# Holding results back while the second chunk of sorted tokens is gathered, and other orders at the attentions' last steps

## What is computed

```python
x = x + attention(layernorm(x), ...)
x = x + ffn(layernorm(x), ...)          # of each token:
    probs = softmax(xt @ Wr + br); gate = max(probs); idx = argmax(probs)    # 8 experts
    h = relu(layernorm_affine(xt) @ W1[idx] + b1[idx])                       # 128 -> 512
    y = (h @ W2[idx] + b2[idx]) * gate
```

## Time and profile before

| | |
|---|---|
| median of three runs | 680.22 us (679.19 to 682.71) |
| the profiled execution | 682.75 us, of it the span 681.4 us |
| PE busy | 652.9 us, 96% |
| ACT busy | 535.7 us, 79% |
| DVE busy | 476.1 us, 70% |
| POOL busy | 364.7 us, 54% |
| HBM read, written | 19.93 MB, 44.75 MB |
| mean granted TensorE clock | 0.988 |

### The profile page before, as it was taken

The page is one execution under the profiler, slowest core; times in us unless marked ns, Lnnn a source line. Parts: engine busy times, 40 slices in busy tenths (PEclk is TensorE's granted clock), DMA queues, the critical chain, the costliest instruction groups (busy, mean ns, idle before and its releaser), DMA issues.

```text
span 681.4 us, 17746 instructions
## 1 busy us (share of the span) xinstructions
PE 652.9 (96%) x5406; PEld 550.9 (81%) x5406; DVE 476.1 (70%) x2139; ACT 535.7 (79%) x1776; POOL 364.7 (54%) x678
## 2 busy tenths in 40 slices
PE   6999999999999999999898999999999999989897
PEld 5778888878788887779796788888888888768896
DVE  4767767776777678778553767687778776887643
ACT  4997978887878889666564989898989898885564
POOL 4744535474557555635452545465745575553645
PEclk9999999999999999999897999999999999999989
DMA  8999999998000000214421000000000000030230
GB/s 274 289 305 301 248 287 298 302 298 224 2 9 17 9 1 17 73 47 162 113 58 48 2 2 1 2 2 9 17 11 1 10 25 2 17 109 23 64 103 12
DMA packets 67468, 64.65 MB, mean 95 GB/s; under 512 B 7793, under 2 KB 63998, under 8 KB 67120
## 3 DMA queue, kind: packets, MB, share of 16 engines
q1 hardware_dynamic: 62624, 56.41, 29.7%
q0 software_dynamic: 3136, 6.34, 2.8%
q10 hardware_dynamic: 1616, 0.79, 0.5%
HBM read 19.93 MB, written 44.75 MB: 95 GB/s over the span
## 4 chain that ended last, share of the span: by engine, by line
PE 83%; DVE 7%; ACT 3%; issue 3%; another core or an unknown queue 1%; POOL 1%; DMA 1%; SPq 0%; DVEq 0%; ACTq 0%; POOLq 0%
PE ps L459 16%; PE ps L568 14%; PE ps L605 14%; PE ps L454 10%; PE ps L456 8%; PE ps L455 8%; PE ps L708 5%; PE ps L722 5%; DVE ring L1197 2%; ACT ring L900 2%; PE ps L642 1%; DMA wkn<-in_w_qkv 1%; PE ps L660 1%; ACT f_ht L949 1%
## 5 line engine op out<-in xcount | busy, mean ns | idle before, releaser
L345 POOL TENSOR_SCALAR ring<-ring,rs 128x256 f32<-128x256 f32 (+1 forms) x500 | 219.1, 454 | 216.7 <-DVE rs L1208 216.5
L900 ACT ACTIVATE ring<-ring,mn 128x256 f32<-128x256 f32 (+1 forms) x512 | 244.4, 490 | 0.0
L459 PE MATMUL ps<-ident,ring 128*128 128x128 f32 x896 | 121.4, 275 | 4.3 <-POOL ring L345 2.2
L568 PE MATMUL ps<-qk 64*128 64x256 f32 (+1 forms) x1024 | 115.3, 364 | 0.9 <-DVE mn L1197 0.6
L605 PE MATMUL ps<-pt,v 128*64 128x256 f32 (+1 forms) x1024 | 111.9, 359 | 1.4 <-DVE pt L1224 0.6
L459 PEld LDWEIGHTS ps<-ident,ring 128*128 128x128 f32 x896 | 102.1, 142 | 11.3 <-POOL ring L345 3.5
L900 ACT ACTIVATION_READ_ACCUMULATOR ring<-ring,mn 128x1 f32 x512 | 104.4, 204 | 0.0
L605 PEld LDWEIGHTS ps<-pt,v 128*64 128x64 f32 x1024 | 65.6, 136 | 45.8 <-issue 14.8
L568 PEld LDWEIGHTS ps<-qk 64*128 64x128 f32 x1024 | 82.6, 187 | 19.2 <-issue 10.5
L868 ACT COPY qk<-ps 128x512 f32<-128x512 f32 x128 | 74.9, 586 | 24.1 <-PE ps L456 22.8
L1197 DVE CUSTOM_DVE_ANT_0 ring<-ps,cm 128x128 f32<-128x128 f32 (+1 forms) x256 | 73.6, 351 | 6.3 <-PE ps L568 6.3
(11 more groups left out here) (211 smaller groups left out, 1351.0 us busy)
## 6 DMA issues: line engine op xcount, KB each, us to landing
xs_scratch<-padt SPq DMA_DIRECT2D x16, 2064.0 KB, 22.1
f_xs<-xs_scratch SPq DMA_DIRECT2D x50, 129.0 KB, 2.4
w<-in_W SPq DMA_DIRECT2D x16, 256.0 KB, 6.0
xs_scratch<-padt SPq DMA_DIRECT2D x2, 1677.0 KB, 21.0
T<-in_bias SPq DMA_DIRECT2D x2, 512.0 KB, 7.6
T<-in_bias SPq DMA_DIRECT2D x1, 1024.0 KB, 10.1
bu<-in_w_kv_up SPq DMA_DIRECT2D x1, 1024.0 KB
row<-in_x SPq DMA_DIRECT2D x1, 768.0 KB, 12.2
```

The costliest lines, as they stand in the source:

```text
L345: i = pool.tensor_scalar(ring[:, hh, it, 0:w], ring[:, hh, it, 0:w], rs[:, q], 1.0, ALU.mult, ALU.mult)
L459: return pe.transpose(out, src, ident[:, :])
L568: i = pe.matmul(PS[u % 2][hh][:, 256 * it:256 * it + w], qk[rows, 128 * it:128 * it + 128], qk[rows, 256:256 + w], start=True, stop=True)
L900: i = act.activation(ring[:, hh, it, 0:w], ring[:, hh, it, 0:w], ACT.Exp, bias=mn[:, q], scale=-1.0, accum_out=sm[:, q])
```

## The change

The change has three parts.

1. **Results wait.** At `HOLD` = 5 POOL's `back(5)` first waits for the gathers of groups 3 and 4 (tiles 12 to 15) to have landed.
2. **Token numbers are copied out.** A new buffer `f_tok` holds the token numbers of all tiles of both stages. DVE copies them, one small copy for each group ahead of the group's first `Y`; `back` reads them there. A place of `f_xs` is then free when DVE's `Y` of its tile is done, and SP waits for that (`v_fy`) instead of a result's landing.
3. **Orders.** PE at n = 12: `Y(10)`, XT of tile 12, `Y(11)`, `H(12)`; at n = 13: XT of tiles 13 to 15, `H(13)`. DVE: index part 0 goes from the end of step 59 to step 60 behind `TR`, part 2 from the end of step 61 to step 63 behind `TR`; at s = 61 `weigh(59)` stands between the two score units; at s = 64 `TR` comes first and `keep(58)` last; the routing and placing of s = 66 come at s = 67 behind `TR`. ACT: at s = 64 the copy of tiles 0 to 3 (XT(0)) goes between the two heads' exponentials of unit 62; at s = 65 the exponentials of unit 63 come behind `TR(61)`.

```diff
+HOLD = LAST_POST["place"] - F0 - 2
-INDEX = {59: 0, 60: 1, 61: 2, 63: 3, 65: 4}
+INDEX = {60: 1, 63: 3, 65: 4}
+
+INDEX_TR = {60: 0, 63: 2}
...
+    f_tok = sb("f_tok", [128, 2, NF], U32)
...
         def back(n):
 
+            if n == HOLD:
+                for m in AT_ONCE:
+                    g = GROUP_OF[m]
+                    pool.wait_ge(d_xs[g], 16 * (GROUPS[g][1] - GROUPS[g][0]) * (st + 1))
             pool.wait_ge(v_fy, NF * st + n + 1)
             pool.indirect_dma_start(
-                ys_dram[st], bass.IndirectOffsetOnAxis(ap=f_xs[:, n % NX, 128:129].bitcast(U32), axis=0),
+                ys_dram[st], bass.IndirectOffsetOnAxis(ap=f_tok[:, st, n:n + 1], axis=0),
                 f_ys[:, n % NY, :], None, bounds_check=NT * 128 - 1, oob_is_err=False).then_inc(d_ys[n % NY], 16)
...
             if n in AT_ONCE:
+                if n == F_EACH:
+                    Y(n - 2)
                 XT(GROUP_OF[n])
-                Y(n - 2)
+                if n == F_EACH:
+                    Y(n - 1)
...
         def step(s):
             n = s - F0
-            if NU < s < NU + 2:
-                expo(s - 2)
...
-            if 2 <= s <= NU:
-                expo(s - 2, (0, 1) if s % 2 or s == NU else (0,))
+            if 2 <= s < NU + 2:
+                expo(s - 2, (0, 1) if s % 2 else (0,))
+            if s == NU:
+                XT(0)
+                expo(s - 2, (1,))
...
-            for g in range(NG):
-                if n == max(GROUPS[g][0] - 2, -1) and GROUPS[g][0] not in AT_ONCE:
+            for g in range(1, NG):
+                if n == GROUPS[g][0] - 2 and GROUPS[g][0] not in AT_ONCE:
                     XT(g)
...
+            if n in FIRST_OF:
+                a0, a1 = GROUPS[FIRST_OF[n]]
+                dve.tensor_copy(f_tok[:, st, a0:a1].rearrange("p (n a) -> p n a", a=1),
+                                f_xs[:, a0 % NX:a0 % NX + a1 - a0, 128:129].bitcast(U32))
             V(dve.tensor_tensor(f_ys[:, n % NY, :], y_bank(n)[:, 0:128], first_layer(n)[:, 512:640], ALU.add))
...
-            if s % 2 == 0 and 6 <= s < LAST_KEEP:
+            if s == NU:
+                TR(s - 4)
+            if s % 2 == 0 and 6 <= s < LAST_KEEP and s != NU:
                 keep(s - 6)
...
-            if 4 <= s < NU + 4:
+            if 4 <= s < NU + 4 and s != NU:
                 TR(s - 4)
+            if s in INDEX_TR:
+                index(INDEX_TR[s])
+            if s == NU + 3:
+                routes(s - 1)
...
+                if s == NU - 3:
+                    weigh(s - 2)
                 S(s)
-            if s % 2 and 3 <= s < NU:
+            if s % 2 and 3 <= s < NU and s != NU - 3:
                 weigh(s - 2)
...
-            if s > NU:
+            if s > NU and s != NU + 2:
                 routes(s)
...
+            if s == NU:
+                keep(s - 6)
...
                 if n >= NX:
-                    sp.wait_ge(d_ys[(n - NX) % NY], 16 * (st * len(range((n - NX) % NY, NF, NY)) + (n - NX) // NY + 1))
+                    sp.wait_ge(v_fy, NF * st + n - NX + 1)
```

## The result

The changed kernel takes 692.22 us (median of six runs, 688.62 to 695.26) beside 681.47 us of the kernel before in the same comparison (678.52 to 684.21): 1.0161 of it, 95% interval 1.0116 to 1.0206. It is slower by 1.6%. The profiled execution took 688.62 us, of it the span 687.2 us, the lowest of its six; that of the kernel before was 682.75 us. So the two traces differ by 5.9 us, where the medians differ by 10.7. TensorE was busy for as long as before, on a span longer by 5.8 us.

The account below looks back on a forecast made before the run. It took TensorE, busy 652.9 of 681.4 us, as the bound, with only its gaps and half-clock stretches to win: 4.0 + 3.1 - 2.0 + 2.0 = 7.1 us, of which 6.2 off the median 680.22 gave 674.0 us, range 669.5 to 681.

Parts of the forecast that it names:

- The handover: Second chunk's gathers, tiles 12 to 15: holding results starts first layer 13 earlier, 4.0 us first stage, 3.1 second.
- The burst of held results: Held results leaving in a row after the gathers: between nothing and 3.7 us a stage, taken as 1.0.
- Token copies: Eight small VectorE copies a stage, one for each group: cost nothing, at most 0.2 us a stage.
- The attentions' ends: New orders at the attentions' last steps: win 0.6 us in the first stage and 1.4 in the second, together 2.0.
- the first chunk is late: At the attentions' ends, the wait for tiles 0 to 3 isn't won back: -2 instead of +2, 678 us; chance 0.10.
- The rival of the waits that stay: At the handovers, results cost gathers only their packets' room: 0.2 us won there, 678 us in all; chance 0.22.
- the dear burst: Held results, eight in a row, cost two waits of 3.7 us in each stage: 685.9 us; chance 0.12.

Follow-up runs that it names:

- e1: The changed kernel with a GpSimd pause of about 1.0 us ahead of each of the held results 6 to 12: 701.64 us, ratio 1.0297.
- e8: The kernel before with token copies, SyncE's wait for VectorE and results 5 to 8 about 2.0 us apart, no hold: 675.26 us, ratio 1.0007.
- e3: The changed kernel with planning piece 2 back at the end of step 61: 685.97 us, ratio 1.0046.
- e4: The kernel before with only the hold at result 5 and the token copies, all orders as before: 688.36 us, ratio 1.0079.
- e2: The changed kernel without the wait at result 5, token copies and new orders kept: 688.99 us, ratio 1.0083.
- r1: Comparison on one chip of the kernel before, the changed one, and token copies with results 5 to 8 paced 2.0 us: 672.7, 677.89, 674.91 us.
- r2: Comparison on another chip: the kernel before, 680.85 us, and the same with token copies and results 5 to 8 paced 2.0 us, 679.36 us, 0.9956.

## Why the prediction was wrong

It said 674.0 us, faster. The steps, one by one:

- **The handover, -4.0 and -3.1 us: right in size.** Measured between tile 12 and tiles 16 to 19, 3.5 and 2.7 us. First layer 13 came at 331.60, forecast 330.7; in the second stage at 651.41, forecast 649.5, the difference being that the whole stage was 1.85 us late by then (SyncE's first gather at 645.82, not 643.97). That the unnamed waits come from results in a row was right; that the gathers beside them matter was not (next point). And they are not there each time: in three of the six comparisons the kernel before took 682 to 684 us (681.5 in that of the result), and its two traces there have these waits; in the other three it took 675 us, and neither its two traces there nor those of the kernels beside it have any. Each comparison was on another chip and none came twice, so a difference of the chips is the likely reason, and not shown.
- **The burst of held results, +1.0 a stage: the term that failed.** It measured 6.05 and 6.80 us in B. I took it nearer to nothing "since the gathers are nearly over by then". That had no part in it: e1 has the same gathers and no late signal beside its spaced results, and late ones in its row from 352.58 on. What counts is how fast results leave, and the hold makes a longer row (seven, and eight in the second stage) than the one that it takes apart (six with the two row writes). The bound I had written, 3.7 us a stage, was one wait of an engine, in a row that TensorE spent partly in a wait for tile 12 anyway. In the middle of steady work nothing hides it: B's 6.05 us are 4.36 of TensorE's idle, and most of the other 1.7 is the half clock, at which TensorE then worked until 344.2. The decision point of that rival, 4.5 us a stage, was passed in both stages.
- **Token copies, nothing: right.** They take 0.15 to 0.20 us each, and e8, which has them, is the same as the kernel before.
- **The attentions' ends, -2.0: the second failure.** The walk was right: tile 3 forecast at 292.0, the transposes came at 291.48 after 2.99 us idle (2.63 in the second stage). What it passed on was not: I let it be taken up by TensorE's other gaps and priced no clock. GpSimd's scaling waited 4.92 and 5.8 us, tiles 4 to 7 came 0.8 us later than before in the first stage instead of 0.6 earlier, and the clock was at half for 3.4 us behind the wait in the first stage (293.1 to 296.5) and for 6.9 in the second (610.5, still in the wait, to 617.4). Undoing this one move gave back 1.15% of the time, 7.8 us, with the hold in place (e3), and 0.6%, 4.1 us, without it; with piece 2 back, the other orders win 0.85 us in the first stage. That is the rival "the first chunk is late", with its sign right and its size (4 us in all) between the same as and half of what was found.
- **The rival of the waits that stay.** Its premise holds: results did not slow the gathers. Tile 12's transpose starts 2.40 us after its issue with results beside it and 2.21 without, a difference of the order of their packets. The rule of the Trainium skill ("DMA: Bandwidth & Descriptors", Queues, rings and completion order), turns between queues by packet, agrees with this, and says nothing of the signals of TensorE, where the time went.
- **The sum** of cases took one rival at a time (and its low end, 4.0 + 3.1 + 3.4 off 680.2, is 669.7 and not 669.5). Here both came true together, the late chunk and the dear burst, which I had given 0.10 and 0.12 and no joint price.

How the 10.7 us between the medians are shared is known only roughly: the hold has 0.8% by e4 and the orders and copies 0.8% by e2, but taken apart the other way round piece 2 alone has 1.15% and the hold 0.2%. In the two traces of the result, of the lowest of the changed kernel's executions, the handovers alone account for the difference: A is 6.2 us shorter and B 12.9 longer, a loss of 6.6 us where the spans differ by 5.8.

## What to carry to other kernels

Before work of an engine is held back to be done at once later, ask what a row of it does at the place where it comes out: the price has to be taken for a stretch of steady work, not from where it is hidden today. A move that frees an engine for its next instruction must be walked to the earliest DMA that hangs on what was moved, and a new wait of TensorE is to be priced with the half clock that can come with it (here waits of 2.99 and 2.63 us, and 3.4 and 6.9 us at half clock). Late signals can also blur a reading: the same move was worth 0.6% or 1.15%, by what else was in the kernel. And where the profile names no releaser, take a trace of the same kernel on another chip before explaining it: if the wait is gone there, as here, a change built on it has nothing to win on that chip.

## What was not expected of the hardware

- In three of the comparisons and in that of the result, signals of TensorE reached their waiters late while GpSimd issued indirect DMAs 1.3 us apart, in the changed kernel up to 5.9 us (VectorE at 340.59, for second layer 12 that had ended at 334.70), and came at once where these stood further apart. No late signal of ScalarE's or VectorE's was found in these stretches: VectorE's piece 5 of the planning went on at its pitch of 0.2 us from 330.89 to 333.21 in the changed kernel. Some came through within the row (the one that ScalarE got at 335.61 after 0.72 us of waiting), others about 1 us after its end. Pitches of 1.29 to 1.35 us held them up, with or without a copy of 0.2 us between; at 2.0 us and more none was late. By what path is open: the trace has no row for it.
- It differs from comparison to comparison, each of which had a chip of its own: the kernel before takes 681 to 684 us in some and 675 us in others, by this for the most part as far as the traces show (A 9.2 to 10.1 us against 6.1 to 6.2, and the half clock behind). Of the same two kernels the changed one is 1.6% slower in the result's and 0.3% in r1, which is within what the kernel before came from itself. The same row of issues 1.29 us apart held up nothing there. Why they differ is open.
- A copy of 128x4 elements on GpSimd took 0.20 us, and 0.66 to 1.03 us where VectorE worked on 128x1024 operands at the time (r2 and e8, 327.4 to 331.1).
